# Variances from squares summed on ScalarE, and output weights centred once, in a fused cross-attention and expert kernel

## The reference

```
h     = layernorm(x)
q,k,v = h Wq^T + bq, ctx Wk^T + bk, ctx Wv^T + bv     16 heads of 32
p     = softmax over 64 tokens of q k^T / sqrt(32), clipped to +-50, masked
delta = (p v) Wo^T + bo
delta = rs * delta                                    rs: a number in 0..0.3
x1    = x + layernorm(delta) * gamma + beta           mean, var over 512, eps 1e-5
n     = layernorm(x1)
g     = softmax(n router^T), kept for the 2 largest of 8 experts
out   = x1 + sum_e g_e * (silu(n down_e^T) up_e^T)    8 experts, 16 wide
```

## Time and profile before

| | us |
|---|---|
| median of 3 runs (lowest, highest) | 227.47 (227.44, 227.49) |
| the profiled execution, its own time | 228.51 |
| its span, from the first to the last instruction | 226.8 |
| busy in the span: PE | 190.2 (84%) |
| DVE | 168.8 (74%) |
| ACT | 92.6 (41%) |
| POOL | 92.6 (41%) |

### The profile page before, as it was taken

The page is one execution under the profiler, slowest core; times in us unless marked ns, Lnnn a source line. Parts: engine busy times, 40 slices in busy tenths (PEclk is TensorE's granted clock), DMA queues, the critical chain, the costliest instruction groups (busy, mean ns, idle before and its releaser), DMA issues.

```text
span 226.8 us, 3663 instructions
## 1 busy us (share of the span) xinstructions
PE 190.2 (84%) x1288; PEld 141.0 (62%) x1288; DVE 168.8 (74%) x355; ACT 92.6 (41%) x164; POOL 92.6 (41%) x150
## 2 busy tenths in 40 slices
PE   0379979979998999999999996699993799973762
PEld 0258858536575886767786871578652688862741
DVE  2873752558859898798875986798599997899694
ACT  2444267516467323575511345722064250424140
POOL 5604059990284335440012260002259852654050
PEclk9999999999999999999999999999999599996599
DMA  6899500247033021000330000033012320110015
GB/s 212 271 398 335 223 3 1 71 144 264 12 95 103 4 56 48 0 3 1 107 98 7 3 0 0 12 107 93 0 48 94 140 94 3 48 46 0 1 61 217
DMA packets 12006, 19.40 MB, mean 86 GB/s; under 512 B 2258, under 2 KB 4306, under 8 KB 11988
## 3 DMA queue, kind: packets, MB, share of 16 engines
q1 hardware_dynamic: 11392, 19.16, 25.0%
q10 hardware_dynamic: 596, 0.01, 0.1%
HBM read 14.45 MB, written 4.72 MB: 85 GB/s over the span
## 4 chain that ended last, share of the span: by engine, by line
PE 75%; DVE 11%; DMA 5%; ACT 4%; issue 3%; SPq 1%; DVEq 0%
PE ps_r L374 52%; PE ps_t L398 6%; PE ps_v L512 6%; DMA wk<-wk_t 5%; PE ps_r L444 4%; PE ps_v L458 3%; ACT stage L707 2%; PE ps_v L471 2%; DVE xs L1024 2%; PE ps_v L515 2%; DVE attt_lo L963 1%; DVE x1t_lo L949 1%; DVE n_st L1027 1%; PE ps_v L511 1%; DVE v_sb L979 1%
## 5 line engine op out<-in xcount | busy, mean ns | idle before, releaser
L374 PE MATMUL ps_r<-hst_hi,wq_hi 128*128 128x512 f32 x64 | 26.1, 408 | 1.6 <-ACT stage L707 1.6
L374 PE MATMUL ps_r<-wo_hi,attt_lo 128*128 128x512 f32 x64 | 25.3, 395 | 0.0
L374 PE MATMUL ps_r<-hst_hi,wq_lo 128*128 128x512 f32 x64 | 25.3, 395 | 0.0
L374 PE MATMUL ps_r<-wo_hi,attt_hi 128*128 128x512 f32 x64 | 25.3, 395 | 0.0
L374 PE MATMUL ps_r<-wo_lo,attt_hi 128*128 128x512 f32 x64 | 25.2, 394 | 0.0
L374 PE MATMUL ps_r<-hst_lo,wq_hi 128*128 128x512 f32 x64 | 25.2, 394 | 0.0
L1330 POOL TENSOR_TENSOR xs<-xs,beta_bc 128x512 f32<-128x512 f32 x16 | 20.9, 1323 | 7.4 <-ACT hs L689 7.4
L512 PE MATMUL ps_v<-dr_hl,x1t_hi 128*128 128x272 f32 x64 | 19.5, 366 | 1.9 <-DVE x1t_lo L949 1.5
L707 ACT ACTIVATE stage<-ps_r 128x1024 f32<-128x1024 f32 x16 | 15.8, 1022 | 8.7 <-PE ps_r L444 8.7
L1354 POOL TENSOR_TENSOR xs<-up_out,xs 128x512 f32<-128x512 f32 x12 | 17.3, 1459 | 3.6 <-ACT up_out L745 3.6
L1335 POOL TENSOR_SCALAR d_ve<-d_mv,rs_sq 128x1 f32<-128x1 f32 x16 | 4.2, 265 | 35.5 <-DVE d_mv L1013 35.3
(11 more groups left out here) (115 smaller groups left out, 467.4 us busy)
## 6 DMA issues: line engine op xcount, KB each, us to landing
wk<-rz_scratch SPq DMA_DIRECT2D x32, 128.0 KB, 2.6
out<-xs SPq DMA_DIRECT2D x16, 256.0 KB, 2.0
xs<-x SPq DMA_DIRECT2D x3, 1024.0 KB, 7.5
xs<-x SPq DMA_DIRECT2D x2, 512.0 KB, 4.2
wk<-wk_t SPq DMA_DIRECT2D x1, 1024.0 KB, 10.6
stage<-wq_t SPq DMA_DIRECT2D x1, 1024.0 KB, 12.8
xs<-wv_t SPq DMA_DIRECT2D x1, 1024.0 KB, 14.9
xs<-wo_t SPq DMA_DIRECT2D x1, 1024.0 KB, 16.9
```

The lines of the kernel that those rows point to most:

```text
L374: last = pe.matmul(dst, w, m, start=start and i == 0, stop=stop and i == n - 1)
```

## The change

The mean of a projected row is taken out beforehand: with the rows of Wo^T and the bias bo each less its own mean, every projected row has mean zero, and its variance is the sum of its squares over 512. So:

- at the start DVE centres Wo (`centre_wo`, four chunks: BN_STATS, BN_AGGR, subtract) and bo (three instructions);
- `projected_squares` (ACT) sums the squares of a projected tile out of PSUM; `scaled` (DVE) multiplies the bank by gamma rs, and waits for the squares;
- `residual` (DVE) is one instruction, which also gives the sum of x1; `x1_squares` (ACT) sums the squares of sum - 512 x1, which is 512^3 times the variance;
- `att_lo` goes from DVE to POOL;
- PE gets 14 matmuls (`WARM`) ahead of everything, which nobody reads; the small loads go from ACT's queue to SP's, Wo is loaded last, and the orders and rings of all engines are written anew.

```diff
+            def projected_squares(b, t):
+                n = NT * b + t + 1
+                act.wait_ge(mm_full, ring_r.count(f"W{b}{t}", every=True))
+                if b:
+                    act.wait_ge(d_ve_ok, n - NT)
+                    act.wait_ge(n_sq_ok, n - NT)
+                act.activation(cen[:, t, :], ps_r[ring_r.bank(f"W{b}{t}")][:, :], ACT.Square,
+                               accum_out=d_sq[:, t:t + 1]).then_inc(d_sq_ok, 1)
+            def x1_squares(b, t):
+                n = NT * b + t + 1
+                act.wait_ge(x1_ok, n)
+                if b:
+                    act.wait_ge(n_ve_ok, n - NT)
+                act.activation(cen[:, t, :], xs[:, bass.ds(NT * b + t, 1), :], ACT.Square, bias=n_sum[:, t:t + 1],
+                               scale=-float(H), accum_out=n_sq[:, t:t + 1]).then_inc(n_sq_ok, 1)
...
-            def centre(b, t):
+            def scaled(b, t):
...
-                hold(mm_full, ring_r.count(f"W{b}{t}", every=True))
-                dve.bn_stats(d_st[:, t, :], bank[:, :]).then_inc(d_st_ok, 1)
-                hold(d_st_ok, n)
-                dve.bn_aggr(d_mv[:, t, :], d_st[:, t, :]).then_inc(d_mv_ok, 1)
-                dve.wait_ge(d_mv_ok, n)
-                dve.scalar_tensor_tensor(cen[:, t, :], bank[:, :], d_mv[:, t, 0:1], gamma_rs[:, :],
-                                         ALU.subtract, ALU.mult).then_inc(mm_free, 1)
+                dve.wait_ge(d_sq_ok, n)
+                dve.tensor_tensor(cen[:, t, :], bank[:, :], gamma_rs[:, :], ALU.mult).then_inc(mm_free, 1)
...
-                dve.scalar_tensor_tensor(x_tile, cen[:, t, :], d_rstd[:, t:t + 1], x_tile, ALU.mult, ALU.add
-                                         ).then_inc(x1_ok, 1)
-                hold(x1_ok, n)
-                dve.bn_stats(n_st[:, t, :], x_tile).then_inc(n_st_ok, 1)
-                hold(n_st_ok, n)
-                dve.bn_aggr(n_mv[:, t, :], n_st[:, t, :]).then_inc(n_mv_ok, 1)
+                dve.scalar_tensor_tensor(x_tile, cen[:, t, :], d_rstd[:, t:t + 1], x_tile, ALU.mult, ALU.add,
+                                         accum_out=n_sum[:, t:t + 1]).then_inc(x1_ok, 1)
...
+            def centre_wo(c):
+                if c == 0:
+                    dve.wait_ge(wo_in, 16)
+                dve.bn_stats(w_st[:, c, :], wo_raw[:, c, :]).then_inc(w_st_ok, 1)
+                hold(w_st_ok, c + 1)
+                dve.bn_aggr(w_mv[:, c, :], w_st[:, c, :]).then_inc(w_mv_ok, 1)
+                dve.wait_ge(w_mv_ok, c + 1)
+                dve.tensor_scalar(wo_raw[:, c, :], wo_raw[:, c, :], w_mv[:, c, 0:1], None, ALU.subtract
+                                  ).then_inc(wo_mid_ok, 1)
...
+            pe.wait_ge(average_ok, 1)
+            for _ in range(WARM):
+                pe.matmul(ps_r[3][:, 0:P], average[:, :], average[:, :], start=True, stop=True)
             pe.wait_ge(ident_ok, 1)
             hs_transpose(0, 0)
...
-            spread(0, 0)
             load(2)
             load(3)
+            spread(0, 0)
```

More of the change, by code:

```diff
@@ L542, in _ @@
             query(0, 1)
+            query(0, 2)
+            values(0)
+            values(1)
             expert_means()
-            scores(0, 0)
-            query(0, 2)
             query(0, 3)
@@ L586, in _ @@
             query(2, 3)
[L587 to L597 removed]
+            hs_transpose(3, 0)
+            down(0, 0)
+            scores(2, 0)
+            hs_transpose(3, 1)
+            hs_transpose(3, 2)
+            project(1, 0)
+            project(1, 1)
+            project(1, 2)
+            sums(2, 0)
             hs_transpose(3, 3)
@@ L659, in _ @@
             down(3, 3)
+            up(2, 0)
+            up(2, 1)
             hid_transpose(3, 0)
@@ L1180, in _ @@
-            centre(0, 2)
-            centre(0, 3)
-            x1_lo(0, 1)
+            residual(0, 2)
+            scaled(0, 3)
             product(1, 0)
             product(1, 1)
-            att_lo(1, 0)
-            residual(0, 2)
+            product(1, 2)
+            product(1, 3)
+            hs_lo(3, 0)
+            clip(2, 0)
+            hs_lo(3, 1)
             residual(0, 3)
             add_cross(0, 0)
+            hs_lo(3, 2)
+            clip(2, 1)
+            scaled(1, 0)
+            residual(1, 0)
@@ L1189, in _ @@
+            scaled(1, 1)
+            scaled(1, 2)
+            reciprocals(2, 0)
+            hs_lo(3, 3)
+            product(2, 0)
+            product(2, 1)
+            scaled(1, 3)
+            x1_lo(0, 1)
+            x1_lo(0, 2)
+            clip(2, 2)
+            clip(2, 3)
+            x1_lo(0, 3)
             add_cross(0, 1)
             largest(0, 0)
-            att_lo(1, 1)
-            x1_lo(0, 2)
-            clip(2, 0)
-            clip(2, 1)
+            reciprocals(2, 1)
             gating(0, 0)
-            product(1, 2)
@@ L1197, in _ @@
-            product(1, 3)
-            att_lo(1, 2)
-            x1_lo(0, 3)
-            add_cross(0, 2)
-            att_lo(1, 3)
-            reciprocals(2, 0)
-            clip(2, 2)
-            clip(2, 3)
-            hs_lo(3, 0)
+            residual(1, 1)
+            x1_lo(1, 0)
+            clip(3, 0)
+            clip(3, 1)
+            product(2, 2)
+            product(2, 3)
+            reciprocals(3, 0)
+            clip(3, 2)
+            clip(3, 3)
+            add_cross(0, 2)
@@ L1269, in _ @@
+            residual(2, 1)
+            largest(1, 0)
+            hid_lo(0, 1)
+            gating(1, 0)
+            add_cross(1, 2)
+            residual(2, 2)
+            add_cross(1, 3)
+            residual(2, 3)
+            largest(1, 1)
+            x1_lo(2, 1)
+            hid_lo(1, 0)
+            add_cross(2, 0)
+            gating(1, 1)
             x1_lo(2, 2)
             x1_lo(2, 3)
-            add_cross(2, 0)
+            scaled(3, 0)
+            residual(3, 0)
             add_cross(2, 1)
+            hid_lo(1, 1)
@@ L1405, in _ @@
             pool.wait_ge(sum_ones_ok, 2 * NT)
-            for c in (2, 3):
+            for c in range(2):
                 pool.wait_ge(wq_hi_ok, c + 1)
@@ L1428, in _ @@
             add_beta(2, 0)
+            att_lo(0, 0)
+            att_lo(0, 1)
             add_beta(2, 1)
```

608 lines of the change are left out of this document (308 added, 300 removed), and 8 rows, old and new, of the table RING_R.

## The result

| | us |
|---|---|
| after, median of 4 runs (lowest, highest) | 215.33 (213.15, 215.79) |
| before, median of 4 runs beside them | 227.48 (227.44, 227.59) |
| ratio (95% interval) | 0.945 (0.938 to 0.951) |
| forecast | 205.4, range 200 to 217 |
| the profiled execution after, and its span | 215.31, 212.8 |

A forecast was written before the change was run, and what follows sets the result against it. PE was taken to bound two thirds, later DVE's slow x1 hand-over. 23.4 start + 155.8 PE work + 5.5 holes = 184.7; plus tail 20.0 = 204.7 span; plus 1.7 less 1.04 = 205.4 us, range 200 to 217.

The forecast's parts named there:

- PE bounds, and late DVE's hand-over; the change takes DVE's load away: Whole kernel: PE binds for two thirds, later DVE handing over x1 tiles; DVE goes from 168.8 to 133 us.
- PE's work by paces: Whole kernel: PE's work summed from full-clock paces, 179.6 us, of which 155.8 from first query to last projection's end.
- Squares at 0.69 to 0.87: ACT: 32 passes of squares at 0.69 us, up to 0.18 more each with a read of the sum; 22.1 to 27.8.
- The beginning costs nothing and gives nothing: Start, before the queries: warm-up, moved small loads and late Wo taken at 0 us, with 2.3 gain as the end.
- The warm-up: Start: 14 matmuls taken at 0, the clock falling before the keys; rival that it carries, 203.1 us, chance 0.17.
- Six small transfers now stand on SP ... so they delay nothing: Start: six small loads between Wq and Wv on SP, whose queue is backed up there, claimed to cost no delay.
- Holes of 5.5 us to the last projection: First query to last projection's end: PE idle 5.5 of 155.8 us at the earlier 4.0 of 113.6; bounds 2 and 13.5.
- the rule and the row: DVE beside POOL: shared SBUF port rule and `gate` at 1.18 against 0.18; each att_lo could hold DVE 1.0, 16 us.
- A tail of 20.0: Last projection's end to span's end: 26.3 us less 1.8, 2.7 and 1.8 is 20.0; bounds 18 and 24.5.
- the weakest of the three terms: Tail, last gating: 1.8 us saved if POOL has its additions behind or ahead of two stretched small instructions.
- The first, at 214.6: Late stretch: DVE's waits become waits for ACT and POOL, holes and half the clock loss stay; 214.6 us, chance 0.25.
- The convoy on ACT: ACT's order: squares queue behind x1 squares, a ps_r bank stays taken, PE stops; four stops give 235.8 us, chance 0.07.

The follow-up runs named there:

- POOL reads nothing: The changed kernel with POOL's 16 att_lo and 12 add_up replaced by MEMSETs of about the same total length, which read no SBUF: 207.69 us, ratio 0.913.
- the additions late: The changed kernel with POOL's four additions of batch 2 held until the last gating's multiply is through: 215.92 us, ratio 0.948.
- the stores ordered too: The changed kernel with batch 2's additions on POOL held, add_up(2,3) on DVE and the last eight stores queued as their tiles get ready: 211.88 us, ratio 0.934.
- four kernels: The changed kernel with hid_transpose(1,0) behind project(3,0), alone 215.81 us, with reordered tail 215.08; with room made on DVE and ACT too, 215.94 and 214.93.

## Why the prediction was right in direction and 9.9 us short

- *PE bounds, and late DVE's hand-over; the change takes DVE's load away.* Right. Putting the statistics back gives 203.6 us from query to end, the value of the kernel before.
- *PE's work by paces.* Nearly right: from the first query to the end of the last projection PE is busy 158.9 us by the windows, for 155.8 by the paces. 1.7 of the difference are the half clock, 1.4 stay unexplained (the same check in the prediction was 1.1 short on the kernel before).
- *Squares at 0.69 to 0.87.* Right, a little cheaper: 0.60 and 0.72, with reads of the sum of 0.2 that begin before the pass ends; ACT 111.8 against 90.5 without them. The groups:

```profile
L771 ACT ACTIVATE hs<-xs,n_sum 128x512 f32<-128x512 f32 x16 | 11.5, 718 | 1.6 <-DVE xs L1072 1.6
L761 ACT ACTIVATE hs<-ps_r 128x512 f32<-128x512 f32 x16 | 9.5, 597 | 26.6 <-PE ps_r L383 26.6
L761 ACT ACTIVATION_READ_ACCUMULATOR hs<-ps_r 128x1 f32 x16 | 3.1, 197 | 0.0
```

- *The beginning costs nothing and gives nothing.* The warm-up: right, and for the reason given, since the clock fell before the keys. The step "Six small transfers now stand on SP ... so they delay nothing" looked at SP alone. With them off ACT's queue Wk landed earlier in every profile, and the first query is 2.4 us earlier (20.99 against 23.42): 1.8 are Wk's landing, 0.65 a shorter first half of the keys (5.85 against 6.50 us), which varies by more than that between kernels with the same start.
- *Holes of 5.5 us to the last projection.* This is the first step that failed. It ended at 188.24; 188.24 - 20.99 - 155.8 leaves 11.4 us, 5.9 too many. The 11.4 are the 4.8 us of the first window, the 3.5 us hole, 1.7 of half clock behind it and the 1.4 above. Where POOL reads nothing the same stretch (19.86 to 181.78) leaves 6.1, near the 5.5 of the forecast: the share of holes was right but for the hold. I had the rule and the row, and priced the hold against DVE's total: "16 us, DVE at 149, still under 169; the sum above would stay". DVE's total was nearly that, 144.5, and it was beside the point: a hold costs where PE waits for the held instruction, and three `att_lo` in a row fell on one gating. The Trainium skill ("SBUF — State Buffer", section "Who interferes with whom") has the pair of ports held for a whole instruction, by a GpSimd operation that reads SBUF against a VectorE one with two SBUF inputs. The traces agree for such VectorE instructions, with 1.19 against 0.18 us, and none of it beside MEMSETs. The clip, a TENSOR_SCALAR with a single SBUF input, is held too (1.08 us mean, 0.75 before), and beside MEMSETs as well (1.71 us).
- *A tail of 20.0.* The second step that failed: it took 24.6 us (188.24 to 212.8). I had taken off 1.8 for holds in the last gating though POOL kept four additions there; the weakest of the three terms, as said, and they stayed (2.7 us over a free gating). With them half clock came back for the last six matmuls, 1.2. A term was missing too, the eight last stores, 2 MB at some 380 GB/s. Where POOL reads nothing the tail still takes 22.1 us, and from 200 to 202 no engine works while the DMA moves 379 GB/s. With the additions late the gating is free and the time from query to end stays at 192.0; with the stores ordered too it is 189.8.
- *Sum.* -2.4 (start) + 5.9 + 4.6 (tail) + 0.8 (the profiled execution lies 2.5 above its span, not 1.7) + 1.0 (the median isn't below it) = 9.9.
- *The rivals.* The first, at 214.6, has the value, and half the mechanism: POOL's holds on DVE grew, but PE doesn't wait for a longer hand-over through ACT. With POOL's reads gone the time is 207.7 at unchanged hand-overs. That its value is met within 1 us is luck: it puts all of its 9.2 us ahead of the last projection, where 5.9 came, and the rest came in terms that it doesn't have. The convoy on ACT did not come: no wait of PE for a bank that squares had yet to read.
- *The signs.* The 3.52 us hole, with `down(2,0)` between it and `project(3,0)`, is about what the prediction named as wrong, a hole of over 3 us in front of a projection of batches 1 to 3. In front of those of batches 1 and 2 there is none.

What stays open: how much of the 7.6 us between after and the kernel in which POOL reads nothing is the two gatings (3.5 and 2.35 us of waits and the clock behind) and how much the other holds (DVE is busy 10.2 us less there, of which these two gatings are 6.3); why keys(0) varies as it does with the same start; and whether the late hole can be had by moving POOL's additions instead of PE's waits.

## What to carry to other kernels

Work moved from a loaded engine to an idle one must be priced at what it does to the instructions beside it, at the places where the bounding engine waits, and not at the sum over the kernel: instructions of 0.2 us in a chain of eight are the ones to look at. If a held chain is on the critical path, take the other engine's work away from it; moving the wait gave nothing in four kernels. Look at what ends last once a tail is shortened (here the queue of stores), and compare variants from a mark behind the loads, where the start of a run varies more than the effect.
